# Causal and first cross attention: projections in three one-pass products, output projections two places later, parts of rows made by ScalarE and VectorE

## The reference

```
h = ln(x, ln1);  q, k, v = split(h @ qkv_w.T + b);  x += attend(q, k, v, causal) @ proj_w.T + b
h = ln(x, ln2);  q = h @ q_w.T + b;  k, v = enc @ k_w.T + b, enc @ v_w.T + b
x += attend(q, k, v) @ ca_proj_w.T + b
x += gelu(ln(x, ln3) @ fc_w.T + b) @ proj_w.T + b
attend(q, k, v) = softmax(q k^T / 4 [+ causal mask]) v      # per head, 512 x 512
```

## Time and profile before

| | |
|---|---|
| median of 3 runs (lowest to highest) | 3852.06 us (3849.43 to 3855.76) |
| the profiled execution | 3852.05 us, span 3850.0 us |
| busy: TensorE, VectorE, ScalarE, GpSimd | 3597.5, 2780.0, 2462.6, 2135.4 us |
| mean granted TensorE clock | 0.959 |
| SELF0 / CROSS0 / MLP0 / CROSS1 | about 0 to 501, 501 to 947, 947 to 1184, 1184 to 1650 us |
| SELF2 / CROSS2 / MLP2 / SELF3 | about 1650 to 2200, 2200 to 2680, 2680 to 2900, 2900 to 3850 us |

### The profile page before, as it was taken

The page is one execution under the profiler, slowest core; times in us unless marked ns, Lnnn a source line. Parts: engine busy times, 40 slices in busy tenths (PEclk is TensorE's granted clock), DMA queues, the critical chain, the costliest instruction groups (busy, mean ns, idle before and its releaser), DMA issues.

```text
span 3850.0 us, 69127 instructions
## 1 busy us (share of the span) xinstructions
PE 3597.5 (93%) x21778; PEld 2047.4 (53%) x21778; DVE 2780.0 (72%) x6841; ACT 2462.6 (64%) x5254; POOL 2135.4 (55%) x2103
## 2 busy tenths in 40 slices
PE   6999999999998999999999999999899999999998
PEld 3444444444884343333333344444787777777776
DVE  3666677875676788789999978876666666666665
ACT  2555567776333777678888877777225666666665
POOL 3465444432344555468998744332436767776765
PEclk7999999998997999989999899998999999999999
DMA  4433353431003434333222244431100000000000
GB/s 104 103 85 81 80 112 86 89 86 45 20 1 66 111 84 90 74 75 86 64 67 61 59 98 92 90 84 49 46 6 6 12 7 13 12 12 7 12 1 12
DMA packets 135373, 220.50 MB, mean 57 GB/s; under 512 B 42720, under 2 KB 44640, under 8 KB 133216
## 3 DMA queue, kind: packets, MB, share of 16 engines
q1 hardware_dynamic: 135008, 216.02, 24.6%
HBM read 59.69 MB, written 5.51 MB: 17 GB/s over the span
## 4 chain that ended last, share of the span: by engine, by line
PE 57%; DVE 14%; POOL 13%; issue 6%; ACT 5%; DMA 4%; SPq 1%; POOLq 0%; DVEq 0%; ACTq 0%
PE MX L703 16%; PE L L703 13%; PE OUT L703 12%; PE ST L703 11%; DVE mx L1523 3%; POOL prob L1968 3%; DVE h_lo L1566 2%; DVE h_hi L1564 2%; POOL prob L2040 2%; DMA sums<-spread 1%; PE L L928 1%; ACT prob L1262 1%; DVE MX L1516 1%; POOL lo L1958 1%; POOL misc L1911 1%
## 5 line engine op out<-in xcount | busy, mean ns | idle before, releaser
L1262 ACT ACTIVATE prob<-ST 128x512 f32<-128x512 f32 (+3 forms) x2304 | 1151.3, 567 | 428.8 <-PE ST L703 423.9
L1523 DVE TENSOR_REDUCE mx<-MX 128x1 f32<-128x512 f32 x1536 | 964.3, 683 | 194.3 <-PE MX L703 193.5
L703 PE MATMUL MX<-stk 48*128 48x512 f32 (+3 forms) x2560 | 902.9, 443 | 78.2 <-DMA stk<-lo 29.2
L703 PE MATMUL ST<-stk 50*128 50x512 f32 (+3 forms) x2560 | 925.1, 446 | 2.4 <-ACT prob L1262 1.0
L703 PEld LDWEIGHTS MX<-stk 48*128 48x128 f32 x2560 | 423.3, 192 | 669.6 <-DVE mx L1523 246.2
L2040 POOL TENSOR_SCALAR prob<-prob,mx 128x128 f32<-128x128 f32 (+3 forms) x512 | 558.5, 1104 | 273.8 <-DVE mx L1714 273.8
L703 PE MATMUL OUT<-prob,V 128*32 128x512 f32 (+3 forms) x5120 | 671.7, 598 | 8.1 <-POOL prob L1975 4.5
L703 PEld LDWEIGHTS ST<-stk 50*128 50x128 f32 x2560 | 427.7, 191 | 54.0 <-DVE prob L1532 17.7
L1516 DVE CUSTOM_DVE_ANT_0 MX<-MX,W_even 128x512 f32<-128x512 f32 x512 | 347.6, 701 | 38.2 <-PE MX L703 37.6
L1968 POOL TENSOR_TENSOR prob<-prob,W_odd 128x512 f32<-128x512 f32 x256 | 324.3, 1283 | 79.6 <-ACT prob L1262 79.4
L1520 DVE CUSTOM_DVE_ANT_0 MX<-MX,later 128x128 f32<-128x128 f32 (+3 forms) x512 | 238.1, 519 | 124.8 <-PE MX L703 124.0
(11 more groups left out here) (238 smaller groups left out, 7587.7 us busy)
## 6 DMA issues: line engine op xcount, KB each, us to landing
stk<-hi SPq DMA_DIRECT2D x640, 128.0 KB, 3.8
stk<-lo SPq DMA_DIRECT2D x320, 128.0 KB, 3.9
misc<-misc SPq DMA_DIRECT2D x160, 128.0 KB, 2.6
sums<-spread SPq DMA_DIRECT2D x80, 256.0 KB
ctx_full<-in_ctx_t SPq DMA_DIRECT2D x24, 512.0 KB, 7.0
W_even<-in_w SPq DMA_DIRECT2D x2, 2048.0 KB, 10.7
XH<-in_ctx_rows SPq DMA_DIRECT2D x8, 512.0 KB, 3.6
X<-in_x_t SPq DMA_DIRECT2D x1, 3584.0 KB, 14.6
```

The lines of the kernel that those rows point to most:

```text
L703: return nc.tensor.matmul(o, l, r, start=start, stop=stop)
L1262: nc.scalar.activation(prob_at(k)[:, q0:S], STB[k % RING][:, q0:S], ACT.Copy if addmask else ACT.Exp).then_inc(ex_done, 2 if addmask else 1)
L1523: nc.vector.tensor_reduce(m, bank[:, :], AX.X, ALU.max).then_inc(mx_red, 1)
```

## The change

- K, Q, V and O of SELF0 and Q and O of CROSS0 become three one-pass products of parts.
- The parts of the normalized rows are made where the transposes are copied out: ScalarE writes the high part from `L` ahead of the full copy (`normalized`), VectorE subtracts after the tiles of places 1 and 2 (`low_part`). CROSS1 does so too, and its `normed_parts` on GpSimd goes, but for batch 0.
- GpSimd makes the parts of the scaled output (`output_parts`) in SELF0 and CROSS0 as well. Weight parts: SELF0's by ScalarE and VectorE at the start, those of Q and O of CROSS0 by GpSimd in slot 14 of SELF0.
- O0 moves from place 7 to 9 and O1 from 9 to 10, in all stages with `AT[False]`: SELF0, CROSS0, CROSS1, CROSS2.
- MLP0's weights are loaded in two halves, the second in the last slot of CROSS0. New tensors lie where weights are not needed at the time.

```diff
-AT = {False: dict(T1=0, M1=1, K0=2, K1=3, Q=5, V0=7, O0=7, M0=8, V1=9, O1=9, T0=10, invert=3, combine=2),
+AT = {False: dict(T1=0, M1=1, K0=2, K1=3, Q=5, V0=7, O0=9, M0=8, V1=9, O1=10, T0=10, invert=3, combine=2),
...
+        odd_up, even_up = hot + 4 * (2048 - WCOLS), hot + 4 * (2048 - 2 * WCOLS)
+        hT_hi = {x: nc.alloc_sbuf_tensor_at(f"hT_hi_{x}", [P, NC, S], F32R, offset=at)
+                 for x, at in (("later", pr_at + 4 * 3072), ("first", sums_at), ("layer0", odd_up))}
         hT_lo = nc.alloc_sbuf_tensor_at("hT_lo", [P, NC, S], F32R, offset=hot + 4 * 32768)
...
+        raw_hi = {x: nc.alloc_sbuf_tensor_at(f"raw_hi_{x}", [P, 2, S], F32R, offset=at)
+                  for x, at in (("early", odd_up), ("last", pr_at + 4 * 3072), ("layer0", odd_up + 4 * 1024))}
+        self_hi = nc.alloc_sbuf_tensor_at("self_hi", [P, 4, NC, E], F32R, offset=even_up)
+        self_lo = nc.alloc_sbuf_tensor_at("self_lo", [P, 4, NC, E], F32R, offset=hot - 8 * WCOLS)
+        ends_hi = nc.alloc_sbuf_tensor_at("ends_hi", [P, 2, NC, E], F32R, offset=even_up)
+        out_hi = nc.alloc_sbuf_tensor_at("out_hi", [P, NC, E], F32R, offset=odd_up)
...
+        PARTS_NO = {SELF0: 0, CROSS0: 1, CROSS1: 2}
+        SELF_ORDER = (1, 0, 2, 3)
...
+        def normed(sa, ba):
+
+            return hT_hi["layer0" if sa != CROSS1 else "later" if ba else "first"], hT_lo
+
+        def produced(so, last):
+
+            return raw_hi["layer0" if so != CROSS1 else "last" if last else "early"], raw_lo
+
+        def weight_parts(so, m, last=False):
+
+            if so == SELF0:
+                return self_hi[:, m, :, :], self_lo[:, m, :, :]
+            if m in (1, 2):
+                return kv_hi[:, m - 1, :, :], kv_lo[:, m - 1, :, :]
+            return out_hi[:, :, :] if last else ends_hi[:, m // 3, :, :], signs[:, m, :, :]
...
-                n = WCOLS if s in MLP_NO else WCOLS // 2
-                sp.dma_start(W[s % 2][:, 0:n], wts[s]).then_inc(w_in[s], 16)
+                n = WCOLS if s == MLP2 else WCOLS // 2
+                sp.dma_start(W[s % 2][:, 0:n], wts[s][:, 0:n]).then_inc(w_in[s], 16)
...
+                    if (s, u) == (CROSS0, UNITS - 1):
+                        sp.wait_ge(ends_low, 3)
+                        sp.wait_ge(l_full, L_NO[s, u - 1, "O1"] + 1)
+                        sp.dma_start(W[0][:, 2048:4096], wts[MLP0][:, 2048:4096]).then_inc(w_upper, 16)
...
+                    if so in PARTS_NO:
+                        source, w = produced(so, last_batch), weight_parts(so, 3, last_batch and so == CROSS0)
+                        for n, (x, y) in enumerate(THREE):
+                            for k in range(2):
+                                last = mm(Lt[:, t, :], source[x][:, k, tok], w[y][:, k, :], n == 0 and k == 0, n == 2 and k == 1)
                         continue
...
+                                elif sa == SELF0:
+                                    self_weights(ba, 1)
...
+                                    if sa == SELF0:
+                                        pe.wait_ge(h_low, NC * ba + cc + 1)
...
-                            if sa == CROSS1:
-                                pe.wait_ge(h_low, NC * (ba + 1))
+                            if sa in PARTS_NO:
+                                pe.wait_ge(h_low, NC * (NB * PARTS_NO[sa] + ba + 1))
                             elif half == 0:
                                 pe.wait_ge(l_free, L_NO[s, u, "T1"] + 1)
+                            if sa == SELF0:
+                                self_weights(ba, 0)
+                            if (sa, ba) == (CROSS0, 0):
...
+                                    project_signs(0, half, normed(sa, ba), cc)
+                                elif sa in PARTS_NO:
+                                    project_parts(weight_parts(sa, 0), half, normed(sa, ba), cc)
...
+                                    elif sa in PARTS_NO or cross_a:
+                                        project_values_parts(weight_parts(sa, 2), source, part, t)
...
+                                if (s, u) == (SELF0, 2):
+                                    pe.wait_ge(self_low, 4)
+                                if (s, u) == (CROSS0, 2):
+                                    pe.wait_ge(ends_low, 2)
...
+                def self_weights(ba, m):
+
+                    if ba == 0:
+                        pe.wait_ge(self_low, SELF_ORDER.index(m) + 1)
...
-                    project_out(s - 1, j)
+                    if s == MLP0 and j == 0:
+                        pe.wait_ge(ends_low, 3)
+                    project_out(s - 1, j, True)
...
-                def normalized(sa, u, c):
+                def normalized(sa, ba, u, c):
 
                     job = L_NO[s, u, ("T0", "T1")[c]]
                     act.wait_ge(l_full, job + 1)
+                    if sa in PARTS_NO:
+                        nc.scalar.activation(normed(sa, ba)[0][:, c, :], L[:, :], ACT.Identity, **scale_shift(sa, c)).then_inc(h_high, 1)
                     nc.scalar.activation(hT[:, c, :], L[:, :], ACT.Identity, **scale_shift(sa, c)).then_inc(l_free, 1)
+
+                def self_weights():
+
+                    act.wait_ge(w_in[SELF0], 16)
+                    for m in SELF_ORDER:
+                        if m == 0:
+                            act.wait_ge(wq_scaled, SCALED[SELF0])
+                        nc.scalar.activation(self_hi[:, m, :, :], wq(SELF0, m), ACT.Copy).then_inc(self_high, 1)
 
...
+            def low_part(sa, ba, c):
+
+                nc.vector.tensor_tensor(hT_lo[:, c, :], hT[:, c, :], normed(sa, ba)[0][:, c, :].bitcast(F32),
+                                        ALU.subtract).then_inc(h_low, 1)
...
+                        for at, m in enumerate(SELF_ORDER):
+                            dve.wait_ge(self_high, at + 1)
+                            nc.vector.tensor_tensor(self_lo[:, m, :, :], wq(SELF0, m), self_hi[:, m, :, :].bitcast(F32),
+                                                    ALU.subtract).then_inc(self_low, 1)
+                            if at < NC:
+                                dve.wait_ge(l_free, L_NO[s, u, f"T{at}"] + 1)
+                                low_part(s, 0, at)
...
+                        if half == 0 and u >= 0 and on["a"] and sa in PARTS_NO and r in (1, 2):
+                            dve.wait_ge(l_free, L_NO[(*kq_slot(U + 1), "T0") if r == 1 else (s, u, "T1")] + 1)
+                            low_part(sa, a_of(s, u, b)[1], r - 1)
...
-                    if s == CROSS1 and u >= 0 and half == 0 and on["a"] and a_of(s, u, b)[0] == s:
-                        for kind, job in enumerate((L_NO[s, u - 1, "T0"], L_NO[s, u, "T1"])):
-                            pool.wait_ge(l_free, job + 1)
-                            normed_parts(b + 1, kind)
...
+                    if (s, u) == (SELF0, UNITS - 2):
+                        pool.wait_ge(l_full, L_NO[s, u - 1, "V1"] + 1)
+                        pool.wait_ge(wq_scaled, SCALED[CROSS0])
+                        for end in range(2):
+                            nc.gpsimd.tensor_copy(ends_hi[:, end, :, :], wq(CROSS0, 3 * end)).then_inc(ends_high, 1)
+                            pool.wait_ge(ends_high, end + 1)
+                            nc.gpsimd.tensor_tensor(signs[:, 3 * end, :, :], wq(CROSS0, 3 * end), ends_hi[:, end, :, :].bitcast(F32),
+                                                    ALU.subtract).then_inc(ends_low, 1)
+                    if (s, u) == (CROSS0, UNITS - 2):
+                        pool.wait_ge(l_full, L_NO[s, u - 1, "Q"] + 1)
+                        nc.gpsimd.tensor_copy(out_hi[:, :, :], ends_hi[:, 1, :, :].bitcast(F32)).then_inc(ends_low, 1)
...
-                        into_parts = (s - 1 if u == 0 else s) == CROSS1
+                        made = s - 1 if u == 0 else s
+                        into_parts = made in PARTS_NO
                         nc.gpsimd.tensor_tensor(raw[:, 1 - half, :], raw[:, 1 - half, :], sums[:, 1 - half, :],
                                                 ALU.mult).then_inc(raw_scaled if into_parts else at_ready, 1)
                         if into_parts:
-                            output_parts(UNITS - 1 if u == 0 else u - 1)
+                            output_parts(made, UNITS - 1 if u == 0 else u - 1)
                     if on["a"]:
                         split(u, U, half, 1)
...
-                def output_parts(v):
-
-                    high, low = (x[:, v % 2, :] for x in (raw_hi[v // 2 == NB - 1], raw_lo))
-                    pool.wait_ge(raw_scaled, v + 1)
+                def output_parts(made, v):
+
+                    high, low = (x[:, v % 2, :] for x in produced(made, v // 2 == NB - 1))
+                    N = UNITS * PARTS_NO[made] + v
+                    pool.wait_ge(raw_scaled, N + 1)
                     nc.gpsimd.tensor_copy(high, raw[:, v % 2, :]).then_inc(raw_high, 1)
-                    pool.wait_ge(raw_high, v + 1)
+                    pool.wait_ge(raw_high, N + 1)
```

51 lines of the change are left out of this document (28 added, 23 removed).

## The result

| | before | after |
|---|---|---|
| median (lowest to highest), 4 runs each | 3852.55 us (3849.43 to 3855.76) | 3905.60 us (3898.98 to 3908.81) |
| profiled execution, its span | 3852.05, 3850.0 us | 3908.81, 3907.1 us |
| mean granted clock | 0.959 | 0.948 |

The account below looks back on a forecast made before the run. The chain from GpSimd's product through the split of Q to `mrows` was taken to bound the slots, not TensorE's work. SELF0 +13, CROSS0 +8, CROSS1 -7 and smaller terms gave +18 us on 3852: 3870 us, range 3825 to 3892.

Parts of the forecast that it names:

- GpSimd's list: SELF0 and CROSS0: the output's copy and subtraction put up to 2.04 us a slot between product and split of Q.
- the odd slot: SELF0: split of Q ends at 334.7, next slot's first tile at 341.0; the slot takes 27.2 us against 25.3.
- the chain: GpSimd's product, split of Q, SP queue, landing of `mrows`; 6.3 us from the split's end to the next slot's first tile.
- I put 0.8 us a batch for them.: SELF0: slow-clock spells brought by new waits of 2 to 2.5 us a slot, partly hidden at the slot's end.
- The slot takes the greater, 27.8: SELF0, even slot: the chain ends at 27.8 us, TensorE's own work at 25.2, so the chain sets the slot.
- 64 x 0.30: SELF0: 64 projection jobs of K, Q, V and O, each 0.30 us less TensorE work in parts.
- +8: CROSS0: even slot +1.3 us from M1 1.34, parts 2.04 and 6.3; odd slot's chain fits; 8 x 1.0 us.
- -7: CROSS1, even slot: moving O0 gains 1.6 us, less 0.6 for M1; seven slots.
- at most 0.3 a batch: CROSS2, which gets only the move: cost of VectorE's residual sum before the odd slot's first tiles, free where a wait covers it.
- Every new wait brings slow clock: Rival: waits of 2 us or more in SELF0 and CROSS1 slots each cost 1.1 to 1.5 us; 3890 us, chance 0.08.
- TensorE decides: Rival: the chain has room for the 2.04 us, so TensorE's saving counts; 3806 us, chance wholly or in part 0.27.
- Blocking of VectorE and GpSimd: Rival: VectorE's SBUF subtractions and GpSimd's instructions exclude each other, 16 in SELF0 on the path; 3880 us, chance 0.05.

Follow-up runs that it names:

- run 8: The kernel before with output projections two places later and GpSimd making the product's parts in SELF0 and CROSS0, read by nothing: 3892.3 us, ratio 1.0104.
- run 9: The kernel of run 8 with the split of Q ahead of the product in SELF0, CROSS0 and CROSS1: 3847.2 us, ratio 0.9991.
- run 4: The changed kernel with GpSimd's split of Q ahead of the product and its parts in every slot: 3908.7 us, ratio 1.0136.
- run 6: The changed kernel with GpSimd's split of Q ahead of the product in SELF0, CROSS0 and CROSS1 only: 3899.9 us, ratio 1.0113.
- run 13: The kernel of run 9 with GpSimd's parts of the product in SELF0 one place later, behind the clear of tile 5: 3845.9 us, ratio 0.9984.
- run 3: The changed kernel with float32 output projections in SELF0 and CROSS0, Q, K and V still in parts: 3888.8 us, ratio 1.0085.
- run 1: The kernel before with only the output projections moved two places later: 3850.3 us, ratio 0.9986.
- run 5: The changed kernel with ScalarE copying the float32 rows out of `L` first, then making the high part from them: 3901.5 us, ratio 1.0130.
- run 12: The kernel before with later projections and split of Q first in CROSS0 and CROSS1, CROSS0's Q and O in parts, all parts by GpSimd: 3822.3 us.
- run 11: The kernel before with, in CROSS1 only, later projections, split of Q first, and rows' parts made by ScalarE and VectorE: 3827.5 us, ratio 0.9946.
- run 2: The changed kernel with the output projections back at places 7 and 9: 3931.7 us, ratio 1.0195.
- run 14: The changed kernel with split of Q first in SELF0, CROSS0, CROSS1, SELF0's product parts behind clear 5, float32 copy first, CROSS2's projections at 7 and 9: 3866.6 us.

## Why the prediction was right and where it failed

**Right: that GpSimd's list decides over TensorE's saving, and the odd slot.** Run 8 shows it: the parts alone, with no cheaper matmul and no other edit but the move, which by itself changed nothing in all, make the kernel 42 us slower. The pieces of the chain measured as forecast: 6.4 us from the split's end to the first tile (forecast 6.3), the odd slot 27.2 (27.2).

**Failed, in SELF0: "I put 0.8 us a batch for them."** This was the term for slow clock behind the new waits. With it failed "The slot takes the greater, 27.8" for the even slot: TensorE's own work was to end at 25.2 and the chain at 27.8, but in seven of eight batches TensorE's work, at half clock for 10 to 17 us, ends that slot, at 30.6 to 32.4 us. So waits for `mrows` stand in 7 slots of SELF0, not in most, and a batch takes 54.2 to 63.9 us, 58.6 in the mean, not 55 to 56. TensorE's waits of over 0.3 us there grew from 22.9 to 38.2 us in sum, but the half-clock time from 43 to 131. What a microsecond at half clock costs can be read twice: in run 9's CROSS1 a batch of 51.5 us with none is 53.2 with 3.4 us of it, 0.5 each; runs 4 and 6 give 19.4 us for about 50, 0.4. The extra 88 us thus cost 35 to 44, an estimate. Waits +15, slow clock +35 to +44, TensorE's cheaper jobs -19 by the forecast's own 64 x 0.30: 31 to 40, measured 35.5. Per batch the slow clock cost 4.4 to 5.5 us where I put 0.8. I had priced one spell from one row and assumed that a wait at a slot's end hides it; the spells fall in the even slot, from 355 and from 372, and the second lies on O0 and the tiles around it. The Trainium skill (TensorE: Matmul & The Clock Gate, HAM oscillation) prices a spell at half its length. The two readings, 0.4 and 0.5, agree with it as an upper end.

**Incomplete: the chain.** Of the 34 us of run 8 in SELF0, 12.5 went with the split in front (run 9). The clears were in the prediction only as a place where the same wait might show. They are a second consumer of GpSimd's list: TensorE's waits for them grew from 4.5 to 20.2 us with the change, more than those for `mrows` (1.3 to 11.2). What they cost by themselves stays open: with the clears ahead of the parts (run 13) their waits halved and the profiled SELF0 was 14 us shorter, but not the median.

**CROSS0: +14 instead of +8, and for another reason.** I charged the chain with most of it. The trace after has 8.7 us of waits at M1 there and hardly any for `mrows`, float32 projections gave nothing back (run 3), nor did the split in front (run 4), and unused parts with the split first cost nothing (run 9). What costs is the move, 1.1 us a batch (run 1), and ScalarE's second copies, for which M1 waits and which delay all that follows it by 1.3 us (run 5). TensorE's timeline, after, CROSS0:

```profile
769.93 0.60 PE L987 MATMUL L<-ident,mhl 128*8 128x128 f32 x4 [1.32 <-ACT hT L1294]
```

The wait of 1.1 to 1.5 us was forecast, its slow clock was not: batches of 58.0 to 59.5 with 3.4 to 6.8 us at half clock (56.4 without), 55.1 in run 12, which lacks the copies.

**CROSS1: +1 instead of -7.** The move alone gives the forecast gain (run 1: 7.9 us). The second copies take it back, which I had put at 0.6 us a slot. The waits for the rows of the maxima rise from 8.9 us before to 23.4; only 6.0 of that come with the copies, since the move alone, which ends the waits for `raw_lo` (16.9 us before), brings them to 17.4 (TensorE's waits, run 1, then after):

```profile
PE MX L703 <- DMA stk<-mrows: 17.4, 12, 2.7
```
```profile
PE MX L733 <- DMA stk<-mrows: 23.4, 12, 4.3
```

With the chain out of the way, making the rows' parts on ScalarE and VectorE still costs 15 us in the stage (run 11).

**CROSS2: "at most 0.3 a batch".** Measured 1.1 (8.5 us; run 1 alone 7.1). The cover named for VectorE's sum was not there.

**Rivals.** Every new wait brings slow clock, 3890, had the right mechanism and too small a price. TensorE decides, 3806, is refuted by the result and by run 8, which loses without any change to TensorE's work. Blocking of VectorE and GpSimd is refuted by VectorE's 32 subtractions (shortest, median, longest in ns):

```profile
L1535 DVE TENSOR_TENSOR hT_lo<-hT,hT_hi_layer x32: 679/683/1096, 22.0 to 888.8; 128x512 fp32r<-128x512 f32 x32
```

The median is the free duration; even the longest is 0.4 us over, against 1.63 in the earlier trace rows.

**Open.** The stretch behind CROSS2 is 8 us longer, with unchanged work. In two of its batches VectorE is idle for 5.3 and 5.4 us, for nothing that the profile shows, where it was for 3.0 and 2.6 us before; the first of them after, then before:

```profile
3315.10 0.17 DVE L1803 RECIPROCAL mx<-mx 128x2 f32<-128x2 f32 x1 [5.30 <-issue]
```
```profile
3266.41 0.17 DVE L1714 RECIPROCAL mx<-mx 128x2 f32<-128x2 f32 x1 [3.00 <-issue]
```

All seven kernels with SELF0's Q, K and V in parts (the change, runs 2 to 6 and 14) take 1198.5 to 1204.3 us there; of the ten others nine take 1190.6 to 1194.0 and one (run 8) 1198.2. That idle time can't be the whole cause: in runs 3, 5 and 14 it is 2.5 to 3.2 us, and the stretch is as long. The cause wasn't tried. The shorter start of the change isn't counted as a gain either: it took 61.6 to 66.6 us in those seven and 64.4 to 68.8 in the others. Nor is it settled why the clock falls behind some waits and not behind others of the same length.
